# A graph kernel's segment sums: additions moved from VectorE to GpSimd, with a ScalarE copy out of PSUM in two of six passes

## The reference

```python
m = relu(x[src] + edge_attr);  x = ln(x + (1 + eps) * x + segment_sum(m, dst))
w = dinv[src] * dinv[dst]      # twice: x = segment_sum(w * x[dst], src)
agg = segment_sum(x[src], dst) # twice: agg @ w_rel + x @ w_root + b
x = ln(x + relu(segment_sum(edge_weight * (x @ w3)[src], dst) + b3))
```

## Time and profile before

| quantity | value |
| --- | --- |
| median of 3 runs | 9893.8 us (9879.71 to 9897.39) |
| profiled execution, its own time | 9887.35 us |
| its span | 9885.6 us |
| DVE, PE, POOL, ACT busy | 7177.8, 7068.5, 4237.3, 3856.5 us |
| sum stage of the edge pass, of the weight pass | 667.3, 667.5 us |
| sum stages of the four plain passes | 386.5, 386.1, 386.4, 386.1 us |

### The profile page before, as it was taken

The page is one execution under the profiler, slowest core; times in us unless marked ns, Lnnn a source line. Parts: engine busy times, 40 slices in busy tenths (PEclk is TensorE's granted clock), DMA queues, the critical chain, the costliest instruction groups (busy, mean ns, idle before and its releaser), DMA issues.

```text
span 9885.6 us, 235117 instructions
## 1 busy us (share of the span) xinstructions
PE 7068.5 (72%) x71829; PEld 5632.3 (57%) x71830; DVE 7177.8 (73%) x13458; ACT 3856.5 (39%) x11229; POOL 4237.3 (43%) x3907
## 2 busy tenths in 40 slices
PE   9888887878821778985666566656676666677987
PEld 8665555556611667883346335533564345566887
DVE  6655555555545778998888888888887888777996
ACT  0355555555522675435840683068206830000000
POOL 0477777777731662003630562056204620465000
PEclk9855555565555555556889788878887889555555
DMA  9466666653367996445888788868876888355442
GB/s 331 125 179 179 178 191 180 182 139 79 79 191 253 301 312 191 111 108 183 306 293 281 252 304 292 267 233 304 293 251 216 304 291 269 128 194 187 112 108 68
DMA packets 1133195, 2087.05 MB, mean 211 GB/s; under 512 B 391662, under 2 KB 655086, under 8 KB 1132590
## 3 DMA queue, kind: packets, MB, share of 16 engines
q1 hardware_dynamic: 812062, 1195.55, 41.9%
q0 software_dynamic: 219008, 627.65, 16.5%
q10 hardware_dynamic: 101904, 261.43, 7.9%
HBM read 1191.46 MB, written 892.68 MB: 211 GB/s over the span
## 4 chain that ended last, share of the span: by engine, by line
DVE 28%; issue 25%; DMA 15%; PE 14%; POOL 13%; DVEq 3%; ACT 2%; POOLq 0%; SPq 0%; ACTq 0%
POOL edge_rows L470 13%; DVE WORK L1097 7%; PE psum L818 5%; DMA WORK<-parts_by_slot 5%; DMA BIG<-edge_rows 5%; DVE WORK L1163 4%; DVE BIG L1148 4%; DVE WORK L1158 3%; PE psum L699 3%; DVE WORK L907 3%; DMA WORK<-blocks_by_edge 3%; DMA edge_rows<-WORK 2%; DVE WORK L1099 2%; ACT WORK L627 2%; PE psum L813 1%
## 5 line engine op out<-in xcount | busy, mean ns | idle before, releaser
L497 POOL DMA_INDIRECT messages_in_parts<-WORK,goal x1480 | 1437.3, 971 | 2756.8 <-ACT WORK L627 2435.7
L470 POOL DMA_INDIRECT edge_rows<-WORK x1664 | 1959.9, 1178 | 863.0 <-issue 491.1
L627 ACT CAST WORK<-psum 128x432 bf16<-128x432 f32 (+1 forms) x4440 | 1707.1, 1019 | 872.2 <-PE psum L813 872.0
L813 PE MATMUL psum<-BIG,WORK 128*128 x11840 | 1357.9, 245 | 874.3 <-DVE WORK L1097 393.9
L1097 DVE TENSOR_TENSOR WORK<-WORK,psum 128x1024 bf16<-128x1024 uint8 x1480 | 1690.3, 1213 | 358.2 <-PE psum L813 268.2
L813 PEld LDWEIGHTS psum<-BIG,WORK 128*128 128x128 bf16 x11840 | 806.8, 106 | 1425.2 <-issue 1108.2
L907 DVE TENSOR_TENSOR WORK<-lane_k,slot_part 128x1024 bf16<-128x1024 bf16 x2220 | 1509.5, 680 | 8.6 <-PE psum L813 8.6
L841 PE MATMUL psum<-WORK 128*128 128x144 bf16 x11840 | 1081.9, 246 | 513.5 <-DVE WORK L907 459.6
L504 POOL DMA_INDIRECT whole_messages<-BIG,goal x740 | 832.0, 1124 | 1248.6 <-DVE BIG L1111 622.1
L841 PEld LDWEIGHTS psum<-WORK 128*128 128x128 bf16 x11840 | 939.0, 149 | 656.6 <-issue 348.2
L818 PE MATMUL psum<-BIG,WORK 128*128 x17760 | 958.6, 214 | 388.9 <-issue 204.4
(11 more groups left out here) (175 smaller groups left out, 8490.0 us busy)
## 6 DMA issues: line engine op xcount, KB each, us to landing
WORK<-messages_in_parts SPq DMA_DIRECT2D x1480, 288.0 KB, 4.2
WORK<-parts_by_slot SPq DMA_DIRECT2D x444, 640.0 KB
BIG<-edge_rows SPq DMA_DIRECT2D x148, 1040.0 KB, 7.2
BIG<-whole_messages SPq DMA_DIRECT2D x740, 193.5 KB, 2.4
messages_in_parts<-BIG ACTq DMA_DIRECT2D x37, 2880.0 KB
WORK<-blocks_by_edge SPq DMA_DIRECT2D x416, 256.0 KB
edge_rows<-BIG ACTq DMA_DIRECT2D x1, 76960.0 KB, 244.4
whole_messages<-BIG ACTq DMA_DIRECT2D x37, 1920.0 KB
```

What stands on the lines that cost most here:

```text
L470: pool.indirect_dma_start(rows_dram, bass.IndirectOffsetOnAxis(ap=at_stage[g][:, j:j + 1], axis=0), row_buf[g][:, j, :], None).then_inc(s_ ...
L497: pool.indirect_dma_start(unit_dram, bass.IndirectOffsetOnAxis(ap=goal[1 - d][:, t:t + 1], axis=0), msg[c].rearrange("p k f -> p (k f)"), ...
L627: act.copy(msg[c][:, 3 * b:3 * b + w, :].rearrange("p k f -> p (k f)"), spread_bank(c, 3 * b)[:, 0:w * W3]).then_inc(s_staged[b], 1)
L813: m = pe.matmul(o, select[c % GB][:, k, :], V3[:, ds(b * W3, W3)], start=True, stop=True)
```

## The change

`take_rest` and `add_sum` move from DVE's stream to POOL's, behind POOL's scatters of the pass. On POOL the block registers are filled ten at a time. POOL's addition reads `pair_sum` in SBUF in all passes. To that end, in the edge and weight passes, ACT copies the 128x48 sum from the bank to `pair_sum` (`take_sum`), with a new semaphore `s_taken`. PE now waits for `s_taken` where it waited for `s_added`. On ACT in the edge pass, `take_unit(t)` and `take_sum(t - 4)` alternate in straight-line code, where `take_unit` was a loop by itself.

```diff
+            sum_regs = [pool.alloc_register(f"sum_block{k}") for k in range(RING)]
...
+                def take_rest(t):
+
+                    if kind == "edge":
+                        pool.wait_ge(s_relu, t + 1)
+                    else:
+                        pool.wait_ge(s_gath[t % RING], 16 * (q * PAIRS + t // RING + 1))
+                    wait_past(pool, s_sum, t + (q * BATCHES - (GB - 1)))
+                    pool.tensor_tensor(rest[t % GB], z[t % RING], z_high[t % RING], ALU.subtract).then_inc(s_rest, 1)
+
+                def add_sum(t, b):
+
+                    n, c = t + q * BATCHES, t % RING
+                    if kind == "plain":
+                        pool.wait_ge(s_reduced, (t + plain_before(q)) // 2 + 1)
+                    else:
+                        pool.wait_ge(s_taken, t + 1 + cut_before(q))
+                    wait_past(pool, s_added, n)
+                    o = AGG[:, ds(b * D, D)]
+                    pool.tensor_tensor(o, o, pair_sum[c // 2][:, c % 2, :], ALU.add).then_inc(s_added, 1)
+
+                for t in range(BATCHES + LAG):
+                    if kind != "plain" and t < BATCHES:
+                        take_rest(t)
+                    if t % RING == LAG:
+                        its_block = load_blocks(pool, sum_regs, batch_block[d][0:1, t - LAG:t - LAG + RING])
+                    if t >= LAG:
+                        add_sum(t - LAG, its_block[(t - LAG) % RING])
...
+                def take_sum(t):
+
+                    n, c = t + q * BATCHES, t % RING
+                    act.wait_ge(s_sum, n + 1)
+                    wait_past(act, s_added, n + 1 - RING)
+                    act.copy(pair_sum[c // 2][:, c % 2, :], bank[c % GB][:, 0:D]).then_inc(s_taken, 1)
...
-                            wait_past(pe, s_added, n - (GB - 1))
+                            wait_past(pe, s_taken, i * RING + (c + cut_before(q) - (GB - 1)))
...
                 late = 0 if kind == "plain" else 1
-                for t in range(BATCHES + late + LAG):
-                    if kind != "plain" and t < BATCHES:
-                        take_rest(t)
+                for t in range(BATCHES + 3):
...
                     if kind != "plain" and t < BATCHES:
                         take_low(t)
-                    u = t - late - LAG
-                    if u >= 0:
-                        if u % BLOCKS == 0:
-                            its_block = load_blocks(dve, sum_regs[0:min(BLOCKS, BATCHES - u)], batch_block[d][0:1, u:min(u + BLOCKS, BATCHES)])
-                        add_sum(u, its_block[u % BLOCKS])
```

More of the change, by code:

```diff
@@ L274, in gnn_program @@
                                            sem("sums_added"))
+        s_taken = sem("sums_taken")
         s_var, s_std = sem("variance_ready"), sem("deviation_ready")
@@ L628, in stage_six, with take_unit @@
                                      spread_bank(c, 3 * b)[:, 0:w * W3]).then_inc(s_staged[b], 1)
[L630 to L635, removed]
-                    act.activation(z[c], z[c], ACT.Relu).then_inc(s_relu, 1)
+                def take_unit(t):
+                    c = t % RING
+                    act.wait_ge(s_gath[c], 16 * (q * PAIRS + t // RING + 1))
+                    act.copy(slot_part[DST][:, t, :], z_meta[c][:, 0:K])
+                    act.copy(goal[DST][:, t:t + 1], z_goal[c]).then_inc(s_mcopied, 1)
+                    act.activation(z[c], z[c], ACT.Relu).then_inc(s_relu, 1)
+                def take_sum(t):
[3 more added lines that the diff above has]
+                    act.copy(pair_sum[c // 2][:, c % 2, :], bank[c % GB][:, 0:D]).then_inc(s_taken, 1)
                 def note_unit(i, c):
@@ L653, in note_units @@
                         note_unit(i, c)
-                def take_units(i):
-                    for c in range(RING):
-                        take_unit(i, c)
                 wait_past(act, s_sum, q * BATCHES)
@@ L665, in _ @@
                     rounds(act, PAIRS, note_units)
-                    rounds(act, PAIRS, take_units)
+                if kind != "plain":
+                    for t in range(BATCHES + LAG):
+                        if kind == "edge" and t < BATCHES:
+                            take_unit(t)
+                        if t >= LAG:
+                            take_sum(t - LAG)
                 if q == 0:
@@ L856, in _ @@
             batch_regs = [dve.alloc_register(f"batch_block_v{k}") for k in range(RING)]
-            sum_regs = [dve.alloc_register(f"sum_block_v{k}") for k in range(BLOCKS)]
             done = [0]
@@ L1137, in reduce_pair @@
                                     .rearrange("p (a c f) -> p a f c", a=2, c=3), AX.X, ALU.add).then_inc(s_reduced, 1)
[L1139 to L1156, removed]
-                    wait_past(dve, s_sum, t + (q * BATCHES - (GB - 1)))
-                    v.tensor_tensor(rest[t % GB], z[t % RING], z_high[t % RING], ALU.subtract).then_inc(s_rest, 1)
                 def take_low(t):
```

## The result

The changed kernel takes 9631.5 us as the median of four runs (9621.9 to 9648.1), beside 9895.6 us for the kernel before on the same chip. The ratio is 0.9731, with an interval of 0.9705 to 0.9758: 2.7% faster. I had forecast 1.6% slower. The profiled execution took 9621.87 us, with a span of 9620.2 us.

What follows compares the result with a forecast made beforehand. DVE was taken as the bound, with PE close behind in the edge pass and loads in the plain passes. +330 us for edge and weight passes and -176 for four plain ones gave 10048 us, range 9480 to 10350.

Steps and rivals of the forecast that it cites:

- The second bound of the plain passes: Plain passes: message loads near their own bound behind DVE, 1.79 us a pair at 329 GB/s.
- one-hot 0.60, low 0.47, rest 0.88 and addition 0.20 make 2.15 us a batch: Edge and weight passes: DVE's and POOL's operations exclude each other and add up in full.
- 0.10 for hand-overs: Edge and weight passes: extra us a batch because rest to low crosses engines, giving 2.25 a batch.
- the fillings cost nothing in these stages: Edge and weight passes: POOL's register fillings covered by DVE's one-hot and low; 0.2 us a batch if uncovered.
- The point from which the sign turns: Edge batch of 2.04 us, below which the plain passes' gain wins and the kernel is faster.
- 1.85 us a pair: Plain passes: DVE's pair with POOL's additions, against 1.80 before; 342 us a stage against 386, -176 for four.
- The fillings hide here: Plain passes: POOL's fillings cost nothing, as POOL's own work is 0.4 + 0.4 of 1.85 us.
- The ACT copy: Edge pass: ACT's copy of 48 columns from PSUM, say 0.2 us, hides; ACT has 1.1 us a batch.
- the border case: Rival, edge and weight passes: exclusion only while data flows, 1.9 to 2.0 us a batch, 9827 us; chance 0.13.
- the full exclusion: Main forecast, edge and weight passes: operations exclude each other for their whole length, +330 us for both; chance 0.50.
- POOL subtractions of a constant length well over 0.9 us: Edge and weight stages: sign in the profile after that the price, not the exclusion, was mis-sized.
- DVE to wait in front of `take_low`: Edge and weight stages: sign of a right forecast, DVE waiting for POOL's subtraction, stages of 780 to 900 us.

Runs made afterwards that it cites:

- static_adds: Changed kernel, but in the plain passes DVE makes the additions into fixed block 0, without register fillings; ratio 0.9722, plain stages 333 to 334 us.
- static_dve: Kernel before, but DVE's additions in all six passes go to fixed block 0, without register fillings; ratio 0.971, edge stage 611 us.
- half_load: Changed kernel, but only half of each message is loaded in the plain sum stages; ratio 0.9707, plain stage 322 us.
- low_psum: Changed kernel, but `take_low` reads its second input from PSUM instead of SBUF, with wrong low parts; ratio 0.9517, edge stage 555 us.
- static_pool: Changed kernel, but POOL's plain-pass additions go to fixed block 0, without register fillings; ratio 0.9715, plain stage 307 us.
- rest_only: Changed kernel, but DVE makes the edge and weight additions from PSUM, with fillings, POOL keeping the subtraction; ratio 0.9688, edge stage 654.8 us.

## Why the prediction was wrong, point by point

**What bounds the kernel: half right.** DVE was the bound in both kinds of stage, and the 52 us of fillings in each were read rightly from the idle time in front of the addition: static_adds finds 52 in a plain stage, static_dve 56 in an edge stage. The second bound of the plain passes, "A batch is 288 KB, which at 329 GB/s takes 0.90 us, or 1.79 for a pair", does not exist at that price. The 329 GB/s of the earlier trace rows were what DVE's pace asked for, since a load starts only when a buffer comes free. The same queue gave 340, 355 and 358 GB/s in later stages, and half_load shows that halving the bytes changes nothing.

**The edge and weight passes: right mechanism, wrong size, and this is the step that failed.** It was "one-hot 0.60, low 0.47, rest 0.88 and addition 0.20 make 2.15 us a batch. I add 0.10 for hand-overs". The engines do exclude each other, in both directions, as low_psum shows by taking one input away. But each operation holds the other engine off for less than I put down: one-hot 0.54 or 0.55 instead of 0.60, low 0.42 instead of 0.47, rest 0.69 instead of 0.88, addition 0.15 instead of 0.20. The sum is 1.80. POOL's subtraction alone takes 0.82 and its addition 0.28, so a part of each lies under DVE's work. The 0.10 for hand-overs costs nothing, as the next operation of the other engine is already started and stands waiting. That the fillings cost nothing in these stages was right: 370 by 1.80 are 666 us, and the edge stage takes 664. The 0.45 us too much a batch are 2 x 370 x 0.45 = 333 us. The point from which the sign turns was 2.04 us a batch, and the truth lies on the other side of it.

The rule of the Trainium skill (SBUF — State Buffer, Who interferes with whom), an exclusive lock for the whole instruction, in both directions, whoever comes first, agrees in its directions and in its order. In its extent the measurement decides: of the 0.82 us that the profile gives POOL's subtraction alone, 0.69 hold off DVE. The estimate of 0.84 us for the subtraction, from the Trainium skill, GPSIMD Engine Reference, § 3, agrees with the 0.82 measured, better than my 0.88.

**The plain passes: too dear.** I took 1.85 us a pair, or 342 us. It was 1.66 without fillings and 323 us with them. The additions stop DVE for 0.09 a pair, and not for some 0.2 to 0.4. My "The fillings hide here" was wrong the other way, by 16 us a stage. The waits of the reduction in the first plain stage of the changed kernel (total us, times, longest) show nearly all of it. Before, it waited once in that stage, for 11.8 us at its start:

```profile
DVE WORK L1174 <- PE psum L880: 17.5, 9, 11.1
...
DVE WORK L1174 <- POOL BIG L529: 8.9, 8, 1.1
```

The 11.1 us are the same start. New are 6.4 us in eight waits for PE and 8.9 us in eight waits for POOL's addition to free a pair sum. Together they are 15.3 us, and in static_pool, without POOL's fillings, DVE waits only 0.7 us beyond the start. The two errors together are 4 x 19 = 76 us.

**The ACT copy** hides, as said. ACT is busy 298 of 664 us in the edge stage.

**The account.** 10048 - 333 - 76 = 9639, against 9631 measured. The rival that came true is the one called the border case, with 0.13 of the chance. Its sum of 1.83 was nearly exact, in part by luck: it had the subtraction 0.11 too dear (0.80) and the other three 0.08 too cheap together (0.53, 0.40 and 0.10). What I put on top for hand-overs (1.95 a batch) made its 9827 too high by 111 us, and it shared the 76 of the plain passes. Its condition, that start-ups lie under the other engine's work, I had in hand: on DVE alone an operation of 0.55 us starts 0.47 before the next, so a part of each was seen to overlap. And the earlier trace rows held the number for POOL: its DMA takes 0.97 us alone and ended 0.85 after DVE's operation, so 0.12 of it lay under DVE's operation, as 0.13 of the subtraction does. I read the 0.85 "as if it had to begin anew" and gave the full exclusion 0.50.

**What I said the profile would show.** "POOL subtractions of a constant length well over 0.9 us would say that the price, not the exclusion, was mis-sized" was a bad test. Most of them have 1.27 us, and the price is 0.82. The two engines fell into a fixed order in which nearly every operation has one stretched length, so the constancy says nothing; the shortest row of the line and the lag between ends do. I had also expected DVE to wait in front of `take_low`. It does not: `take_low` starts in time and is stretched to 1.18 us, so the wait counts as busy time.

## What to carry to other kernels

Where DVE operations with both inputs in SBUF meet POOL operations that read SBUF, as in this kernel, budget them as one stream, batch by batch, each at a little less than its length alone (the edge stage's pieces: 1.80 us, the period). Here moving the long subtraction lost (it costs 0.47 us of a batch on DVE, 0.69 from POOL), and moving the short additions won a little (two cost 0.24 us of a pair on DVE, 0.09 from POOL). Giving one input of DVE's operation from PSUM took it out of the sum. Look at idle time called "issue" in front of an address computed from registers: removing or resizing those fillings (30 to 20, one line, ratio 0.9546) was worth more than moving any arithmetic, in the sum stages and in PE's select stages together. A DMA share near 1 is a bound only if half the bytes would change the stage.

## What the runs showed of the hardware

The price of a register filling depends on where its numbers start and on how many they are. On DVE a filling of 30 takes 2.3 and 6.7 us in turn, one of 20 takes 1.35 each time, and one of 10 takes 1.06 and 2.3 in turn; one of 10 on POOL takes 1.03 and 2.3 in turn, one of 20 there 1.3. On PE it is about 2 to 4.8 and 8 to 11.6 us in turn for 30, and 1.4 to 2.7 for 20. Two neighbours of the changed kernel on POOL, the second and the third of the edge stage, both of 10 registers:

```profile
L69 POOLq TENSOR_LOAD <-batch_block x1: 2294/2294/2294, 3819.8 to 3819.8; - x1
L69 POOLq TENSOR_LOAD <-batch_block x1: 1034/1034/1034, 3837.8 to 3837.8; - x1
```

What alternates between them is the start of the piece in its row of 4-byte numbers, here 40 and 80 bytes; the length is the same. Short are the starts at multiples of 80 and of 240 bytes, all multiples of 16, and long those at the odd multiples of 40 and of 120 bytes, which are multiples of 8 only. Since 80 is no multiple of 32, a start at a multiple of 16 bytes of its row is what the short ones share. At such starts 10, 20 and 30 registers cost DVE 1.06, 1.35 and 2.3 us. PE's fillings in the changed kernel, 30 at a time (shortest, median, longest in ns):

```profile
L69 PEldq TENSOR_LOAD <-batch_block x78: 1686/4416/11632, 3131.1 to 8826.9; - x78
```

DVE's addition whose second input is in PSUM (0.19 us in rest_only) was not held up by POOL's subtraction beside it, nor was the reduction of the plain passes, whose one input is in PSUM, by POOL's additions (0.45 us as in the earlier trace rows).
